# Expert feed-forward on one core: the four heads' weights summed by accumulating transfers in place of GpSimd and TensorE

## What is computed

```python
def _L0_ffn_ref(hidden_states, W_up, W_down, W_q, keys, down_embed, up_embed):
    q = einsum(hidden_states, W_q)                      # 4 heads
    sim = einsum(q, keys)                               # two sides, 64 keys each
    # top 8 of each side, their 64 sums, top 8 of those: 8 experts of 1024 a head
    scores, pk = top_k(all_scores, 8)
    indices = take_along_axis(all_idx, pk)
    de, ue = down_embed[indices], up_embed[indices]
    w = silu(einsum('btd,bthkd->bthk', hidden_states, de) * softmax(scores))
    experts_states = einsum('bthk,bthkd->btd', w, ue)
    dense = silu(hidden_states @ W_up.T) @ W_down.T
    return dense + experts_states

x = x + 0.5 * _L0_ffn_ref(_layernorm(x), ...)
```

## Time and profile before

| | us |
|---|---|
| median of 2 runs | 4006.93 (4005.85 to 4008.0) |
| the profiled execution | 4008.62 |
| its span, first to last instruction | 4006.8 |
| mean granted TensorE clock, of full speed | 0.983 |

### The profile page before, as it was taken

How to read it: one execution, slowest core, us unless ns; L and a number is a source line. 1 busy time by engine, 2 the same in 40 slices (tenths; PEclk the granted TensorE clock), 3 DMA queues, 4 the chain that set the end, 5 groups by cost and what they waited for, 6 DMA issues and landing times. The chain is left out here.

```text
span 4006.8 us, 81018 instructions
## 1 busy us (share of the span) xinstructions
PE 3796.5 (95%) x28440; PEld 3314.4 (83%) x28440; DVE 3198.6 (80%) x7738; ACT 3098.6 (77%) x7882; POOL 2701.5 (67%) x2202
## 2 busy tenths in 40 slices
PE   7999999999979999999998799999999997999989
PEld 6888888888858888888886688888888887898878
DVE  7888888888758888888875788888888877756667
ACT  6888888888759999999996688888888877632166
POOL 7888888888655554655541788888888866512266
PEclk9999999999989999999999899999999998999999
DMA  2000000000010000000000100000000003331342
GB/s 66 17 17 17 17 17 17 17 17 17 9 44 18 13 23 14 22 23 13 23 7 18 64 17 17 17 17 17 17 17 17 17 12 98 122 105 53 127 151 90
DMA packets 135061, 141.90 MB, mean 35 GB/s; under 512 B 8672, under 2 KB 131968, under 8 KB 134656
## 3 DMA queue, kind: packets, MB, share of 16 engines
q1 hardware_dynamic: 134656, 136.71, 10.7%
HBM read 80.06 MB, written 56.62 MB: 34 GB/s over the span
## 5 line engine op out<-in xcount | busy, mean ns | idle before, releaser
L300 POOL TENSOR_TENSOR f_grid<-f_sim 128x1024 f32<-128x1024 f32 x512 | 969.4, 1910 | 0.1
L1512 ACT ACTIVATE a_ex<-a_p_s,a_mneg 128x128 f32<-128x128 f32 x2048 | 728.2, 409 | 89.9 <-DVE a_mneg L1566 89.9
L686 DVE SCALAR_TENSOR_TENSOR f_p_u<-f_grid,f_te,f_p_dot 128x1024 f32<-128x1024 f32 x512 | 653.2, 1276 | 111.7 <-PE f_p_dot L106 65.3
L308 POOL TENSOR_TENSOR f_q<-f_q 128x1024 f32<-128x1024 f32 x256 | 607.9, 2386 | 123.1 <-ACT f_q L558 121.0
L695 DVE SCALAR_TENSOR_TENSOR f_q<-f_p_u,f_rz,f_grid 128x1024 f32<-128x1024 f32 x512 | 650.9, 1271 | 0.4
L539 ACT ACTIVATE f_grid<-f_grid,f_negm 128x1024 f32<-128x1024 f32 x512 | 559.2, 1142 | 0.0
L1512 ACT ACTIVATION_READ_ACCUMULATOR a_ex<-a_p_s,a_mneg 128x1 f32 x2048 | 508.8, 248 | 0.0
L443 PE MATMUL f_p_y<-f_eup,f_wT 128*128 128x256 f32 x2048 | 472.9, 379 | 0.0
L438 PE MATMUL f_p_y<-f_wdn,f_hs 128*128 128x256 f32 x2048 | 468.4, 382 | 0.0
L443 PEld LDWEIGHTS f_p_y<-f_eup,f_wT 128*128 128x128 f32 x2048 | 388.5, 190 | 57.7
L438 PEld LDWEIGHTS f_p_y<-f_wdn,f_hs 128*128 128x128 f32 x2048 | 378.8, 190 | 49.7
(11 more groups left out here) (646 smaller groups left out, 11029.3 us busy)
## 6 DMA issues: line engine op xcount, KB each, us to landing
x_f<-f_yt SPq DMA_DIRECT2D x64, 256.0 KB, 2.1
f_xt<-x SPq DMA_DIRECT2D x32, 256.0 KB, 2.9
a_xt<-x_f SPq DMA_DIRECT2D x16, 512.0 KB, 3.8
x_a<-a_yt SPq DMA_DIRECT2D x16, 512.0 KB, 2.9
f_xt<-x_a SPq DMA_DIRECT2D x32, 256.0 KB, 2.9
c_xt<-x_f SPq DMA_DIRECT2D x16, 512.0 KB, 4.7
x_c<-c_yt SPq DMA_DIRECT2D x16, 512.0 KB, 3.1
b1p_xt<-x_c SPq DMA_DIRECT2D x16, 512.0 KB, 3.9
```

What stands on the lines that cost most here:

```text
L300: g_grid.mark(pool.tensor_tensor(grid[v][:, hd, :].rearrange("p (i j) -> p i j", i=XROWS), sx[:, hd, :].unsqueeze(2).to_broadcast([P, XROW ...
L308: g_pair.mark(pool.tensor_tensor(q[v][:, 2 * k, :], q[v][:, 2 * k, :], q[v][:, 2 * k + 1, :], ALU.add), f"{v}{k}")
L686: d_mask.mark(dve.scalar_tensor_tensor(out=p_u[:], in0=grid[v][:, hd, :], scalar=te[:, v, hd, TOP - 1:TOP], in1=p_dot[:], op0=ALU.is_ge, o ...
L1512: last = act.activation(ex[t.step % 2][:, i, n, :], p_s[i][:, n, :], ACT.Exp, bias=mneg[:, i, n:n + 1], accum_out=z[t.step % 2][:, i, n:n ...
```

## The change

In both expert stages the four heads' weights are summed by transfers that accumulate, issued from GpSimd. `summed(t, v, k)` has three steps now: q0 += q1 once `front` is done, q0 += q2 once `clamped` is done, q0 += q3 once `back` is done. The second and third wait for the transfer before, on the semaphores `s_add[v][k]`, which are made outside the stages. Each transfer moves 128 x 1024 fp32, 512 KB. `turn_w` waits for the third and has four plain transposes a group in place of eight accumulating ones. On TensorE three of the four `turn_w` groups of a turn move behind a `dense` or `dots`, and the fourth behind `hidden(t, 0)`; the first `experts` of v=1 moves behind `dots`. On ScalarE the copies `turned` move along: the first of v=0 into `weights(t, 1)`, the second behind `listed(t+1, 0)`, those of v=1 behind `listed(t, 1)` and behind the exponentials of v=1. On GpSimd `scores(t+1, 0, (2,))` and `scores(t+1, 1, (0,))` stand between the first and the second transfer of v=0 and v=1.

```diff
@@ -171,7 +171,7 @@
 HALF = EC // 2
 
 
-def expert_ffn(nc, name, src, dst, w):
+def expert_ffn(nc, name, src, dst, w, s_add):
 
     with ExitStack() as ctx:
         m = Memory(nc, ctx, name)
@@ -230,7 +230,6 @@
         d_mask = m.track("d_mask", *(k for v in range(V) for k in (*parts[HEADS * v:HEADS * (v + 1)], f"{v}tail")))
         d_mul = m.track("d_mul", *parts)
         a_silu = m.track("a_silu", *(f"{k}{v}" for v in range(V) for k in ("front", "third", "tail", "clamped", "back")))
-        g_pair = m.track("g_pair", *(f"{v}{k}" for v in range(V) for k in range(2)))
         t_hid = m.track("t_hid", *(str(k) for k in range(4)))
         a_hid = m.track("a_hid", *(str(k) for k in range(4)))
         t_wT = m.track("t_wT", "00", "01", "10", "11")
@@ -304,9 +303,10 @@
 
                 def summed(t, v, k):
 
-                    a_silu.wait(pool, t, f"back{v}" if k else f"front{v}")
-                    g_pair.mark(pool.tensor_tensor(q[v][:, 2 * k, :], q[v][:, 2 * k, :], q[v][:, 2 * k + 1, :], ALU.add),
-                                f"{v}{k}")
+                    a_silu.wait(pool, t, (f"front{v}", f"clamped{v}", f"back{v}")[k])
+                    if k:
+                        s_add[v][k - 1].wait(pool, t)
+                    s_add[v][k].mark(pool.dma_start(q[v][:, 0, :], q[v][:, k + 1, :], accum_op=ALU.add))
 
                 def tails(t, v):
 
@@ -347,17 +347,20 @@
                         scores(t + 1, 0, (0, 1))
                     clamps(t, 0)
                     summed(t, 0, 0)
+                    if after:
+                        scores(t + 1, 0, (2,))
                     summed(t, 0, 1)
+                    summed(t, 0, 2)
                     tails(t, 1)
                     if after:
-                        scores(t + 1, 0, (2,))
                         pairs(t + 1, 1)
                         scores(t + 1, 0, (3,))
                     clamps(t, 1)
+                    summed(t, 1, 0)
                     if after:
                         scores(t + 1, 1, (0,))
-                    summed(t, 1, 0)
                     summed(t, 1, 1)
+                    summed(t, 1, 2)
                     if (t + 3).exists(last=count):
                         root(t + 3)
                     if after:
@@ -415,15 +418,13 @@
 
                 def turn_w(t, v, k):
                     if k == 0:
-                        g_pair.wait(pe, t, f"{v}1")
+                        s_add[v][HEADS - 2].wait(pe, t)
                     if (v, k) != (0, 0):
                         a_wT.wait(pe, t, f"{v}0" if k else "01")
                     elif (t - 1).exists():
                         a_wT.wait(pe, t - 1, "11")
                     for e in range(HALF):
-                        for hd in (0, 2):
-                            last = pe.matmul(p_wT[:, e, :], q[v][:, hd, (k * HALF + e) * P:(k * HALF + e + 1) * P],
-                                             ident[:], is_transpose=True, start=hd == 0, stop=hd == 2)
+                        last = pe.transpose(p_wT[:, e, :], q[v][:, 0, (k * HALF + e) * P:(k * HALF + e + 1) * P], ident[:])
                     t_wT.mark(last, f"{v}{k}")
 
                 def dense(t, v):
@@ -464,36 +465,35 @@
 
                 def step(t):
                     before, after, later = (t - 1).exists(), (t + 1).exists(last=count), (t + 2).exists(last=count)
-                    if before:
-                        turn_w(t - 1, 1, 0)
                     if after:
                         similar(t + 1, 1)
                     hidden(t, 0)
                     if before:
+                        turn_w(t - 1, 1, 0)
+                        dense(t - 1, 1)
                         turn_w(t - 1, 1, 1)
-                        dense(t - 1, 1)
-                        experts(t - 1, 1, 0)
                     dots(t, 1)
                     if before:
+                        experts(t - 1, 1, 0)
                         experts(t - 1, 1, 1)
                     hidden(t, 1)
                     if later:
                         turn_h(t + 2)
                     hidden(t, 2)
+                    hidden(t, 3)
+                    dense(t, 0)
                     turn_w(t, 0, 0)
-                    hidden(t, 3)
-                    turn_w(t, 0, 1)
-                    dense(t, 0)
                     if after:
                         dots(t + 1, 0)
+                    turn_w(t, 0, 1)
                     experts(t, 0, 0)
                     experts(t, 0, 1)
                     if later:
                         similar(t + 2, 0)
                 turns(pe, count, unroll, step)
-                for k in range(2):
-                    turn_w(end, 1, k)
+                turn_w(end, 1, 0)
                 dense(end, 1)
+                turn_w(end, 1, 1)
                 for k in range(2):
                     experts(end, 1, k)
 
@@ -556,6 +556,8 @@
 
                     d_mul.wait(act, t, f"{v}1")
                     a_silu.mark(act.activation(q[v][:, 0:2, :], q[v][:, 0:2, :], ACT.Silu), f"front{v}")
+                    if v:
+                        turned(t, 0, 0)
                     d_mul.wait(act, t, f"{v}2")
                     a_silu.mark(act.activation(q[v][:, 2, :], q[v][:, 2, :], ACT.Silu), f"third{v}")
                     g_tail.wait(act, t, f"use{v}")
@@ -569,13 +571,15 @@
                 def next_exps(t):
 
                     listed(t, 0)
+                    if (t - 1).exists():
+                        turned(t - 1, 0, 1)
                     exps(t, 0, (0, 1))
                     if (t + 1).exists(last=count):
                         similar(t + 1, 0)
                     exps(t, 0, (2, 3))
+                    listed(t, 1)
                     if (t - 1).exists():
                         turned(t - 1, 1, 0)
-                    listed(t, 1)
 
                 def upper(n):
 
@@ -600,9 +604,9 @@
                 def step(t):
                     before, after, later = (t - 1).exists(), (t + 1).exists(last=count), (t + 2).exists(last=count)
                     exps(t, 1, (0, 1))
+                    exps(t, 1, (2, 3))
                     if before:
                         turned(t - 1, 1, 1)
-                    exps(t, 1, (2, 3))
                     if after:
                         similar(t + 1, 1)
                     hidden(t, 0)
@@ -613,13 +617,12 @@
                     if later:
                         turn_h(t + 2)
                     hidden(t, 2)
-                    turned(t, 0, 0)
                     hidden(t, 3)
-                    turned(t, 0, 1)
                     weights(t, 1)
                     if after:
                         next_exps(t + 1)
                 turns(act, count, unroll, step)
+                turned(end, 0, 1)
                 for k in range(2):
                     turned(end, 1, k)
 
@@ -2267,14 +2270,17 @@
 
 def macaron(nc, out, x, w):
 
-    stages = [(expert_ffn, "f1"), (dilated_attention, "a1"), (expert_ffn, "f2")]
-    src = x
-    for stage, name in stages:
-        dst = nc.dram_tensor(f"x_{name}", (N, D), F32, kind="Internal").ap()
-        stage(nc, name, src, dst, w)
-        src = dst
+    dst = {k: nc.dram_tensor(f"x_{k}", (N, D), F32, kind="Internal").ap() for k in ("f1", "a1", "f2")}
+    with ExitStack() as sems:
+        s_add = {k: [[Track(sems.enter_context(nc.semaphore(f"{k}_s_add{v}{n}")), "added", inc=16)
+                      for n in range(HEADS - 1)] for v in range(V)] for k in ("f1", "f2")}
+        expert_ffn(nc, "f1", x, dst["f1"], w, s_add["f1"])
         clear_semaphores(nc)
-    mix_and_attend(nc, src, out, w)
+        dilated_attention(nc, "a1", dst["f1"], dst["a1"], w)
+        clear_semaphores(nc)
+        expert_ffn(nc, "f2", dst["a1"], dst["f2"], w, s_add["f2"])
+        clear_semaphores(nc)
+        mix_and_attend(nc, dst["f2"], out, w)
 
 
 def layouts(i):
```

## The result

The changed kernel takes 4588.85 us (median of two runs, 4583.71 to 4594.0) against 4006.93 before: a ratio of 1.145, 95% interval 1.140 to 1.151. It is 582 us slower. The profiled execution has a span of 4591.5 us and a mean granted clock of 0.944.

A forecast was written before the change was run, and what follows sets the result against it. TensorE's queue was taken to bound the kernel at 33.29 us a turn; after the change, transfer chains would set 37.9. 4008.6 + 295 for the turns + 17 for the ends = 4321, as a median 4320 us; range 4085 to 4700.

The forecast's parts named there:

- No gain on TensorE: TensorE's queue in an expert turn: floor 33.6 us against 33.29, so no gain even with transfers that cost nothing.
- The three gaps: TensorE waits opened by moving transposes: between the two `similar` 0.83 us, before `hidden(t, 3)` 0.87, before `dense(t, 0)` 0.86.
- the loop through VectorE and ScalarE: From `mask` through `dots`, `hidden` and ScalarE to the next `mask`: 35.05 us even with instant transfers, +1.76 a turn, 113 us.
- L: Time from an accumulating transfer's issue on GpSimd until the next may be issued; taken as 4.5 us, bounds 2.9 and 6.3.
- Loop D: Transfer chains of v=0 and v=1 in one loop: longest, sets the turn at 37.9 us, +4.6 a turn, 295 us.
- Loop B: For v=0, from ScalarE's Silu through three transfers, transposes and TensorE's work to the next Silu: 36.9 us.
- T0: Point the forecast counts from: the end of `similar(t+1, 0)` on TensorE, 400.94 in the profiled turn before.
- Ends: At each expert stage's end nothing hides the last transfer chain: 8.7 us more, 17 for both stages.
- The page's figure: Skill page's estimate for a GpSimd-issued transfer: 2.0 us plus bytes at 436 GB/s, about 3.2 us for 512 KB.
- In time: Rival: transfers up to 3.9 us fit into GpSimd's freed 9.5 us and the 35.05 us loop decides; 4131 us, chance 0.32.
- Slow transfers: Rival: GpSimd's transfers take 5.5 to 6.3 us each, a turn of 42.9 to 46.9, 4640 to 4900 us; chance 0.2.
- Faster: Rival: TensorE stays the bound and ScalarE's three round trips shrink; 3866 us with all three gone, chance 0.04.

## Why the prediction was right

**No gain on TensorE.** Right. The three gaps opened as counted, and without any transfer the new order costs 154 us where the loop through VectorE and ScalarE had said 113: 35.7 us a turn against 35.05.

**The transfers.** Right in mechanism, too small in size: 4320 was forecast and 4589 measured, 313 us and 582 us above before. The term that failed is L = 4.5, the time from one issue to the next. The landing was sized well, 4.6 us against 4.5, but GpSimd's next issue starts about 0.5 later still, and the first transfer of v=0 has SyncE's load and store beside it. Measured are 6.45 and 5.10 for v=0, 5.36 and 5.06 for v=1. Loop D in measured terms: v=0 6.45 + 5.10, to the first of v=1 3.84 (439.08 to 442.92), v=1 5.36 + 5.06, landing and wakening 4.58 (411.57 to 416.15), and from there to the next issue of v=0 11.38 (to 427.53). That is 41.77 us. It had to come out as the turn, since the parts lie end to end; what makes it the loop is that none of them holds slack. GpSimd works without a pause through the 3.84, and ScalarE through the 11.38 from its copy at 416.84 on. With the same terms the forecast had 37.9; of the 3.9 us between, 4.05 are in the five transfers (26.55 for 5L = 22.5), the other terms came out 0.2 shorter. Over 28 turns the means are 6.28, 5.39, 3.85, 5.39, 5.16, 4.83 and 11.36, together 42.25: 4.5 us more than forecast in the five transfers, 0.2 less in the rest.

**Loop B, and a term that was missing.** From the Silu of v=0 to its transposes the forecast had 3L = 13.5, measured are 16.1 (427.53 to 443.65). I had left out the clock: behind a wait of 5 us the granted clock is 0.62 from 402.6 to 407.0, and `dots` costs 1.4 us more and the four transposes before it 0.3. From the transposes to T0 of the next turn it is 10.43 us (401.87 to 412.30, the end of the slot of the product at 412.07) for 8.69. From T0 to the next issue it is 15.12 for 14.7, without the 0.11 that TensorE waits for the chain of v=1. B is 16.12 + 10.43 + 15.12 = 41.67, against 41.78 of D. ScalarE's wait of 0.87 us at 416.84 is no measure of the distance: 0.8 of it was forecast, as the time that TensorE's own queue needs up to these transposes. So the two loops are all but equally long. D is the longer by 0.3 us on the mean, and in 9 of 29 turns of the first stage TensorE does not wait for the chain of v=1 at all, so in these turns B sets the time. The runs agree that shortening B alone is of no use: with the clock restored nothing was gained, with work put into D 2.9 us a turn were lost.

**Ends.** 8.7 us a stage was forecast for the last chain, and that was too much. The first load of the attention stage starts at 1106.20 before and 1395.59 after: 289.4 us, and 32 turns of 9.04 (42.32 less 33.28, the means of the middle turns) make 289.3. In the second expert stage 292.7 us are added, of which the turns make 288.1. So 0 and 5 us are left for the ends where 17 in all had been put. From the last Silu of v=0 to the attention's first load it is 43.0 us instead of 31.8, only 2.1 more than a turn adds. The two stages make up the whole of the 582 us.

**The page's figure.** The Trainium skill (DMA: Bandwidth & Descriptors, Anatomy of one DMA, SWDGE path) gave about 2.0 us plus the bytes at 436 GB/s. The fixed part agrees with the 2.0 that the two sizes leave for no bytes. The rate does not: 262 kB in 1.3 us is about 200 GB/s. That the transfer reads its destination as well, as the forecast assumed, would fit; no run shows it. So 3.2 us by the page were 4.6 on the chip.

**The rivals.** In time (4131): refuted for three in a chain, true for one (4175, whose order costs the 154). Slow transfers of 5.5 to 6.3: the landing was not that slow, but the mean of the five intervals is 5.4, just inside the forecast's own 3.9 to 5.5, and the 4589 measured lie nearer to this rival's 4640 than to the 4320 forecast. (The upper end of the range, 4700 for L = 5.6, would be 4680 by the forecast's own terms.) Faster: in this order it is out even with no transfer at all (4163), though another order does get under before.

## What to carry to other kernels

A transfer that stands in for an engine's addition costs that engine little and its consumer the whole latency: count latencies in a row between the producer's end and the consumer's issue slot, add the idle in which the issuing queue waits for its own previous transfer, and hide one, not three. Before an instruction is moved away from a place, ask what wait it was covering there; the cover is worth as much as the work. And what lies beside the loop that binds gains nothing when it is shortened; the order of the queues, looked for by counting such loops, gave here the 2% that moving the sum did not.

## What the runs showed of the hardware

- An accumulating transfer of 512 KB within SBUF, issued from GpSimd, holds GpSimd 0.85 to 0.95 us and lands after 4.6 us; of 256 KB after 3.3. Another 0.5 us or so pass until an issue that waits for it starts.
- The second of two such transfers 2.4 us apart lands after 4.8 to 4.9 us when nothing else is under way, and after 6.6 with SyncE's two transfers of 256 KB beside them. A single one takes 6.45 us to the next issue beside SyncE's two instead of 5.14, and those land after 5.2 and 5.6 us instead of 2.1 and 3.0.
- Behind TensorE's wait of 5.16 us the granted clock was 0.50 from 401.8 to 402.7 and 0.62 from 402.6 to 407.0, and 1.00 again at 426 to 427; 1.2 GHz is the 0.50 of these numbers, 2.4 GHz the 1.00. Four transposes had a modelled 1.12 us in place of 0.60.
- The instructions of GpSimd behind an issue read 0.3 us longer each, 2.20 for a `scores` instead of 1.91, but their rows overlap. From the start of the `scores` at 440.87 to the next instruction at 442.73 it is 1.86 us, so the longer row costs nothing there.
